# Expert down products cut at 128 rows, with the 48-row pieces of two blocks in the two row halves of the array

## The chip, the cores and the metric

The kernel is one program on one core of one Trainium2 chip. Its engines are TensorE (PE, with its weight loads shown as PEld), VectorE (DVE), ScalarE (ACT), GpSimd (POOL) and SyncE (SP), which run side by side and meet at semaphores. The metric is the device time of one execution in microseconds, the median of several runs.

## What is computed

Four layers follow each other on 2048 tokens of 256 values: a cross attention, a mixture of 64 experts with a shared expert, a second attention and a small mixture of 8. The change is in the second layer, whose reference is, cut to what matters:

```python
def _mlp(x, gw, uw, dw):
    return silu(x @ gw.T) * (x @ uw.T) @ dw.T
rw = _route(x, gate_w, gate_bias)                      # 8 of 64 experts for each token, with weights
expert_out = vmap(lambda gw, uw, dw: _mlp(x, gw, uw, dw))(Wg, Wu, Wd)   # I = 176 inner values each
routed = einsum('eth,te->th', expert_out, rw)
shared = _mlp(x, Sg, Su, Sd)                           # 2 x 176 = 352 inner values
out = routed + shared
```

The down product of an expert is a sum over 176 inner values, and that of the shared expert a sum over 352. The array of PE sums over at most 128 rows in one pass, so each has to be cut. All of it is float32.

## The kernel before

**Blocks.** The tokens of an expert are gathered into half blocks of 64 rows; two half blocks, mostly of one expert or of two neighbours, make a block of 128 rows, and there are 160 blocks (`NRUN`). The first half block of a block (`FIRST`, partitions 0 to 63 of the result) uses the weights of its expert where they were loaded, `wgu` and `wdn`, in one of eight slots (`WSLOT`). The second (`SECOND`, partitions 64 to 127) uses copies, `wguB` and `wdnB`, that DVE and ACT make for each block. A product of `FIRST` takes the left 64 columns of the array and one of `SECOND` the right 64.

**The order on PE.** It is written out by hand, two blocks at a time (`c_group(j)`, j = 0, 2, 4, ...): the down product of block j-3, gate and up products of blocks j and j+1 (`c_up`), the down product of block j-2, then the transposes of the gathered rows of blocks j+2 and j+3 and those of the inner values `hC` of blocks j and j+1. A down product (`c_down`) is four calls: the 176 inner values are cut into two pieces of 88 rows (`IC`), and each piece has one product for `FIRST` and one for `SECOND`, of 64 weight columns by 256 moving columns. In the trace each such call is two matmul records.

**The other engines.** ACT takes the down products out (`c_y_out`, which also scales them), issues the store of the rows (`store_y`), copies the transposed rows (`c_copy_xT`), applies SiLU (`c_gate`) and makes `wdnB` (`second_dn`). DVE multiplies gate and up into `hC` (`c_product`), copies its transpose to `hT` (`c_copy_hT`) and makes `wguB` (`second_gu`). POOL issues the gathers of rows, eight blocks ahead (`gather`), and tells when the weights of a block are there (`weights`, four blocks behind the gather). SP loads the weights of an expert, eight experts ahead, with one DMA for `wgu` and one for `wdn`.

**The shared expert.** Thirteen of the sixteen token tiles go through it while the routing is worked out on DVE (`s_step`: gate and up, the transposes of the tile before, its down product). Three wait until after the last expert block (`l_up`, `l_transpose_h`, `l_down`). Here a tile has 128 rows and one set of weights, so the down product takes all 128 columns; it is four pieces of 88 rows.

Of the kernel before, what the change touches and what calls it, by code (L numbers as in the profile page):

```python
# [14 lines left out]
P = 128  # L15
# [29 lines left out]
IC = I0 // 2  # L45
GU = 2 * I0
NSH = 2
# [58 lines left out]
def bass_flamingo(nc, A, out):  # L106
    with ExitStack() as ctx:  # L107
# [47 lines left out]
        with ExitStack() as region:  # L155
# [6 lines left out]
            scores = s("scores", [P, NT, E0])  # L162
            sfc = s("sfc", [P, NGT, GE])
            t1 = s("t1", [P, NGT, GE])
            t2 = s("t2", [P, NGT, GE])
# [36 lines left out]
            wdnB = s("wdnB", [IC, 2, 2, D])  # L202
# [71 lines left out]
        with ExitStack() as region:  # L274
            s = tensors(region)
            wgu = s("wgu", [P, NSH + WSLOT, DC, GU])
            wdn = s("wdn", [IC, NSH + WSLOT, 2, D])
# [6 lines left out]
            hT = s("hT", [IC, 2, 2, P])  # L284
# [41 lines left out]
        b_trash, b_rw, b_rwd = sem("b_trash"), sem("b_rw"), sem("b_rwd")  # L326
# [8 lines left out]
        c_guB, c_dnB = sem("c_guB"), sem("c_dnB")  # L335
# [84 lines left out]
        FIRST, SECOND = slice(0, HR), slice(HR, P)  # L420
        EARLY_B, LATE_B = slice(0, NT - 4), slice(NT - 4, NT)
# [125 lines left out]
        def _(sp):  # L547
# [20 lines left out]
            sp.dma_start(n1_rows[T:ROWS, :], zero[:]).then_inc(b_trash, 16)  # L568
# [5 lines left out]
            sp.dma_start(wdn[:, 0:NSH, :, :], A["sdn"].rearrange("e (c p) n -> p e c n", p=IC)).then_inc(ld_sh, 16)  # L574
# [8 lines left out]
            def load_dn(e, q):  # L583
                sp.dma_start(wdn[:, NSH + q, :, :], A["wdn"][e].rearrange("(c p) n -> p c n", p=IC)).then_inc(w_ld[q], 16)

            for q in range(WSLOT):
                sp.wait_ge(s_gu, 2 * q + 1)
                load_gu(q, q)
                load_dn(q, q)


            for q in range(WSLOT - 1):
                sp.wait_ge(w_ld[q], 32)
                sp.sem_inc(w_ready, 1)
            sp.wait_ge(b_er, 1)
            with sp.Fori(1, E0 // WSLOT) as i:
                for q in range(WSLOT):
# [4 lines left out]
                    sp.wait_ge(w_ld[last], 32 * i if q == 0 else 32 * i + 32)  # L602
# [3 lines left out]
            sp.wait_ge(w_ld[WSLOT - 1], 32 * E0 // WSLOT)  # L606
# [98 lines left out]
        def _(pool):  # L705
# [32 lines left out]
            power(4, LATE_B)  # L738

# [42 lines left out]
            pool.wait_ge(b_trash, 16)  # L782
            pool.wait_ge(b_st, 16 * XG)
# [56 lines left out]
            pool.wait_ge(const_ready, 3)  # L840
# [162 lines left out]
        def _(act):  # L1003
# [128 lines left out]
            def c_group(j, i, n):  # L1132
# [30 lines left out]
            def l_copy_hT(n):  # L1163
# [4 lines left out]
                act.copy(hT[:], ps[0:IC, 5, :].rearrange("p (f c n) -> p f c n", f=2, c=2)).then_inc(l_hT, 1)  # L1168
# [163 lines left out]
        def _(pe):  # L1332
# [85 lines left out]
            pe.wait_ge(ld_sh, 32)  # L1418
# [1328 lines left out]
```

## Time and profile before

| | |
|---|---|
| median of 3 runs | 1361.5 us (1353.13, 1361.5 and 1361.72) |
| span of the profiled execution, first to last instruction | 1352.5 us; no other time of it is given |
| PE busy | 1232.8 us, 91% of the span |
| DVE, ACT, POOL busy | 913.6, 754.3 and 502.9 us |
| mean granted TensorE clock | 0.974 of full speed |
| HBM | 91 GB/s over the span |

A record of PE has a modelled end, so two neighbouring matmuls seem to overlap; what a matmul costs the engine is the distance from its start to the next start. The busy time of an engine says nothing of whether it is waited for: that is read from the stage in question, from what stood idle before an instruction and what ended it.

### The profile page before, as it was taken

To read this page: it belongs to the slowest core of one execution; us is meant where nothing else is said; L and a number is where in the kernel's file an instruction comes from. 1 tells how busy PE (TensorE), PEld (TensorE's weight loads), DVE (VectorE), ACT (ScalarE), POOL (GpSimd) and SP (SyncE) were. 2 spreads that over 40 slices of the span, in tenths; PEclk is the share of its full clock that TensorE was granted. 3 is DMA by queue.
4 is the path that set the end of the run, shared out by engine and by line. 5 is a ranking of instruction groups with operands and counts; after the bars stand their busy time and mean duration, and the time that the engine had idled before them with its cause. 6 is when DMAs were issued, how large, how long until landed. Compare 5 with 4: busy or idle time off the path is not lost. (4 is left out here: it accounts for less than half of the span.)

```text
span 1352.5 us, 32733 instructions
## 1 busy us (share of the span) xinstructions
PE 1232.8 (91%) x9060; PEld 928.9 (69%) x9062; DVE 913.6 (68%) x2392; ACT 754.3 (56%) x1930; POOL 502.9 (37%) x549
## 2 busy tenths in 40 slices
PE   4999999999999999997578888989878999999998
PEld 3887665555555555554456676767756899999997
DVE  7988857555555555554486876767785766676666
ACT  2444566556565555652447876778764544444443
POOL 1012354333343333424876677774711111011010
PEclk9999999999999999999779999999999999999999
DMA  5013216777576557534432222221200000000000
GB/s 117 0 57 105 78 40 193 228 210 231 174 222 188 172 162 230 179 96 131 131 88 64 67 66 57 63 59 39 96 24 10 16 17 16 16 16 16 8 0 17
DMA packets 99465, 125.02 MB, mean 92 GB/s; under 512 B 28595, under 2 KB 84371, under 8 KB 99347
## 3 DMA queue, kind: packets, MB, share of 16 engines
q1 hardware_dynamic: 62339, 59.05, 15.1%
q0 software_dynamic: 13968, 43.53, 11.6%
q10 hardware_dynamic: 23040, 20.98, 4.6%
q8 instruction: 59, 0.97, 0.3%
q14 instruction: 59, 0.48, 0.1%
HBM read 95.58 MB, written 27.95 MB: 91 GB/s over the span
## 5 line engine op out<-in xcount | busy, mean ns | idle before, releaser
L779 POOL DMA_INDIRECT xg<-n_rows,idx x160 | 163.3, 1021 | 242.3 <-DVE wS L2262 198.7
L1334 PE MATMUL ps<-wgu,xT 128*64 x640 | 202.9, 459 | 0.4 <-ACT xT L1104 0.3
L1334 PE MATMUL ps<-wdn,hT 88*64 (+1 forms) x768 | 199.1, 385 | 4.5 <-ACT hT L1168 2.4
L1334 PE MATMUL ps<-wguB,xT 128*64 128x352 f32 x640 | 202.9, 459 | 0.0
L1212 ACT ACTIVATE pD<-ps,nmx 128x333 f32<-128x333 f32 x256 | 139.2, 547 | 83.7 <-DVE nmx L2443 72.6
L2443 DVE TENSOR_REDUCE nmx<-ps 128x1 f32<-128x333 f32 x256 | 126.2, 496 | 87.1 <-PE ps L1334 86.1
L1334 PE MATMUL ps<-wdnB,hT 88*64 88x256 f32 x640 | 168.4, 386 | 0.0
L1702 PE MATMUL ps<-ident,pD 128*128 128x128 f32 x768 | 135.0, 287 | 35.6 <-DVE pT L2449 33.2
L1334 PEld LDWEIGHTS ps<-wdn,hT 88*64 88x64 f32 (+1 forms) x768 | 104.6, 145 | 74.5 <-issue 43.2
L813 POOL DMA_INDIRECT yg<-y_rows,slotG x128 | 123.3, 963 | 80.8 <-DMA y_rows<-yC 26.4
L1334 PEld LDWEIGHTS ps<-wgu,xT 128*64 128x64 f32 x640 | 87.3, 137 | 85.4 <-issue 73.2
L1702 PEld LDWEIGHTS ps<-ident,pD 128*128 128x128 f32 x768 | 98.7, 146 | 52.5 <-issue 21.0
L1129 ACT ACTIVATE yC<-ps,wS 128x256 f32<-128x256 f32 x160 | 76.0, 475 | 98.4 <-PE ps L1334 97.0
L1334 PE MATMUL ps<-kM,qP 128*128 128x334 f32 x256 | 109.1, 427 | 9.5 <-ACT pD L1212 9.1
L2274 DVE COPY hT<-ps 88x256 f32<-88x256 f32 x160 | 67.0, 419 | 71.9 <-PE ps L1334 67.8
L1300 ACT ACTIVATE sl<-ps 128x256 f32<-128x256 f32 x128 | 48.1, 383 | 104.8 <-PE ps L1334 101.5
L2610 DVE TENSOR_TENSOR gg<-sl,ps 128x256 f32<-128x256 f32 x128 | 52.9, 419 | 77.4 <-ACT sl L1300 76.6
L2262 DVE TENSOR_SCALAR wS<-xg 64x1 f32 x320 | 47.2, 147 | 83.3 <-ACT yC L1129 65.5
L1113 ACT COPY wdnB<-wdn 88x512 f32 x160 | 98.6, 617 | 0.0
L1119 ACT ACTIVATE sg<-ps 128x176 f32<-128x176 f32 x160 | 50.8, 318 | 72.6 <-PE ps L1334 70.5
L1334 PEld LDWEIGHTS ps<-wguB,xT 128*64 128x64 f32 x640 | 87.3, 137 | 0.0
L2255 DVE COPY wguB<-wgu 128x704 f32 x160 | 81.3, 550 | 2.2 <-POOLq L773 2.2
(323 smaller groups left out, 3300.7 us busy)
## 6 DMA issues: line engine op xcount, KB each, us to landing
wgu<-in_wgu SPq DMA_DIRECT2D x64, 352.0 KB
y_rows<-yC ACTq DMA_DIRECT2D x160, 128.0 KB
wdn<-in_wdn SPq DMA_DIRECT2D x64, 176.0 KB
xg<-n_rows,idx POOLq DMA_INDIRECT x160, 3.7
kraw<-in_kD SPq DMA_DIRECT2D x8, 308.0 KB, 2.8
x<-in_x SPq DMA_DIRECT2D x4, 512.0 KB, 5.0
n_rows<-nB SPq DMA_DIRECT2D x4, 512.0 KB, 4.1
yg<-y_rows,slotG POOLq DMA_INDIRECT x128, 4.7
```

The lines of the kernel that those rows point to most:

```text
L779: pool.indirect_dma_start(out=xg[:, b % XS, :], out_offset=None, in_=n1_rows, in_offset=bass.IndirectOffsetOnAxis(ap=idx[:, b:b + 1], axis ...
L813: pool.indirect_dma_start(out=yg[:, q, k, :], out_offset=None, in_=y_rows, in_offset=bass.IndirectOffsetOnAxis(ap=slotG[:, u:u + 1], axis= ...
L1113: act.copy(wdnB[:, n % 2, :, :], wdn[:, bass.ds(slot, 1), :, :].rearrange("p s c n -> p (s c) n")).then_inc(c_dnB, 1)
L1119: act.activation(sg[:, n % 2, :], ps[:, 2 + n % 2, 0:I0], ACT.Silu).then_inc(c_silu, 1)
L1129: act.activation(yC[:, n % YS, :], ps[:, 6 + n % 2, 0:D], ACT.Copy, scale=wS[:, n % XS:n % XS + 1]).then_inc(c_y, 1)
L1212: act.activation(pD[:, k % AHEAD, :], ps[:, score_bank(k), 0:NK1], ACT.Exp, bias=nmx[:, k:k + 1], accum_out=den[:, k // TB // HG1, head_of ...
L1334: return pe.matmul(o, lhsT, rhs, start=start, stop=stop, **kw)
L1702: last = pe.transpose(ps[:, 5 + k % 2, c * P:(c + 1) * P], pD[:, k % AHEAD, at:at + P], ident[:])
L2255: dve.tensor_copy(wguB[:, n % 2, :, :], wgu[:, bass.ds(slot, 1), :, :].rearrange("p s c n -> p (s c) n")).then_inc(c_guB, 1)
L2274: dve.tensor_copy(hT[:, n % 2, :, :], ps[0:IC, 4 + n % 2, 0:2 * P].rearrange("p (c n) -> p c n", c=2)).then_inc(c_hT, 1)
L2443: dve.tensor_reduce(nmx[:, k:k + 1], ps[:, score_bank(k), 0:NK1], AX, ALU.max, negate=True).then_inc(d_mx, 1)
L2610: dve.tensor_tensor(gg[:, f % 2, int(second), :], sl[:, int(second), :], ps[:, f % 4, SEQ:2 * SEQ], ALU.mult).then_inc(f_g2 if second else ...
```

## The change

The 176 inner values of an expert are cut into 128 and 48 instead of 88 and 88. `c_down` now holds only the 128-row piece of a block. The 48-row pieces of two blocks j-3 and j-2 come together in `c_down_rest`, after `c_down(j-2)`: for an even block the piece lies in partitions 64 to 111 and for an odd one in 0 to 47, so that the four products (two blocks, `FIRST` and `SECOND`) stand in four different quarters of the array. `c_dn`, which tells that a down product is done, is raised there for both blocks.

For this the 48 rows of `wdn` are loaded twice, at partitions 0 and 64, and POOL copies them for each block into a new tile `wdnF` of eight places. `wdnB` and `hT` get four places in the place of two. ACT takes out both down products after the gates, in turn with the copies of the transposed rows, and issues both stores at the end. The shared down product is three pieces of 128, 128 and 96 rows in the place of four of 88, and its transposes are three. Of the inner values of an expert block the second transpose has 112 columns (even) or 48 (odd).

The core of the diff:

```diff
-IC = I0 // 2
+IREST = I0 - P
+REST_AT = P // 2
+SHARED_CHUNKS = ((0, P), (P, P), (2 * P, 2 * I0 - 2 * P))
+HTS, FS = 4, 8
+WLOAD = 16 * 4
...
+            wdnB = s("wdnB", [P, HTS, 2, D])
+            wdnF = s("wdnF", [P, FS, D])
...
-            hT = s("hT", [IC, 2, 2, P])
+            hT = s("hT", [P, HTS, 2, P])
...
+        def rest_rows(m):
+            at = REST_AT * (1 - m % 2)
+            return slice(at, at + IREST)
...
-                sp.dma_start(wdn[:, NSH + q, :, :], A["wdn"][e].rearrange("(c p) n -> p c n", p=IC)).then_inc(w_ld[q], 16)
+                sp.dma_start(wdn[:, NSH + q, 0, :], A["wdn"][e][0:P]).then_inc(w_ld[q], 16)
+                for at in (0, REST_AT):
+                    sp.dma_start(wdn[at:at + IREST, NSH + q, 1, :], A["wdn"][e][P:I0]).then_inc(w_ld[q], 16)
...
+            sp.wait_ge(const_ready, 3)
...
+            pool.wait_ge(a_o, NT)
+            pool.wait_ge(a_od, NT)
+            pool.memset(wdn[:, NSH:, 1, :], 0.0).then_inc(const_ready, 1)
...
+                slot = pool.value_load(slot_row[0:1, 0, b:b + 1], min_val=NSH, max_val=NSH + WSLOT - 1)
                 pool.wait_ge(w_ready, need)
                 pool.sem_inc(w_block, 1)
+                if b >= FS:
+                    pool.wait_ge(c_dn, NEARLY + b - FS + 1)
+                pool.tensor_copy(wdnF[:, b % FS, :], wdn[:, bass.ds(slot, 1), 1, :].rearrange("p s n -> p (s n)")).then_inc(c_dnF, 1)
...
-                act.copy(hT[:], ps[0:IC, 4, :].rearrange("p (f c n) -> p f c n", f=2, c=2)).then_inc(s_hT, 1)
+                act.copy(hT_all[:, 0:3 * P], ps[:, 4, 0:3 * P]).then_inc(s_hT, 1)
...
-                act.copy(wdnB[:, n % 2, :, :], wdn[:, bass.ds(slot, 1), :, :].rearrange("p s c n -> p (s c) n")).then_inc(c_dnB, 1)
+                act.copy(wdnB[:, n % HTS, :, :], wdn[:, bass.ds(slot, 1), :, :].rearrange("p s c n -> p (s c) n")).then_inc(c_dnB, 1)
...
-                if inside(j - 3):
-                    c_y_out(j - 3, i, n - 3)
                 if inside(j - 1):
                     second_dn(second[0], j - 1, n - 1)
-                if inside(j - 3):
-                    store_y(j - 3, n - 3)
                 if inside(j):
                     for a in range(GROUP):
                         c_gate(j + a, n + a)
-                if inside(j - 2):
-                    c_y_out(j - 2, i, n - 2)
                 for a in range(GROUP):
+                    if inside(j - 3 + a):
+                        c_y_out(j - 3 + a, i, n - 3 + a)
                     c_copy_xT(j + 2 + a, n + a)
                 if inside(j):
                     second_dn(second[-1], j, n)
-                if inside(j - 2):
-                    store_y(j - 2, n - 2)
+                for a in range(GROUP):
+                    if inside(j - 3 + a):
+                        store_y(j - 3 + a, n - 3 + a)
...
-            def transpose_h(slot, bank, at=0):
-                for c in range(2):
-                    last = pe.transpose(ps[0:IC, bank, at + c * P:at + (c + 1) * P], hC[:, slot, c * IC:(c + 1) * IC], ident[:])
+            def transpose_shared_h(bank):
+                for c, (first, n) in enumerate(SHARED_CHUNKS):
+                    last = pe.transpose(ps[0:n, bank, c * P:(c + 1) * P], h_all[:, first:first + n], ident[:])
+                return last
+            def shared_down(bank):
+                for c, (_, n) in enumerate(SHARED_CHUNKS):
+                    last = mm(ps[:, bank, 0:D], hT_all[0:n, c * P:(c + 1) * P], wdn_all[0:n, c, :], c == 0, c == 2)
                 return last
             def s_down(t, r):
                 after(pe, s_y, t)
                 pe.wait_ge(s_hT, t + 1)
-                for f in range(2):
-                    for c in range(2):
-                        last = mm(ps[:, 6, 0:D], hT[:, f, c, :], wdn[:, f, c, :], f == 0 and c == 0, f == 1 and c == 1)
-                last.then_inc(c_dn, 1)
+                shared_down(6).then_inc(c_dn, 1)
...
             def c_down(m):
-                slot = slots[m]
                 pe.wait_ge(c_dnB, m + 1)
                 pe.wait_ge(c_hT, m + 1)
                 if m == 0:
                     pe.wait_ge(s_y, NEARLY)
                 after(pe, c_y, m - 1)
-                for c in range(2):
-                    mm(ps[FIRST, 6 + m % 2, 0:D], hT[:, m % 2, c, FIRST], wdn[:, bass.ds(slot, 1), c, :], c == 0, c == 1, skip_group_check=True)
-                    last = mm(ps[SECOND, 6 + m % 2, 0:D], hT[:, m % 2, c, SECOND], wdnB[:, m % 2, c, :], c == 0, c == 1, skip_group_check=True)
-                last.then_inc(c_dn, 1)
+                mm(ps[FIRST, 6 + m % 2, 0:D], hT[:, m % HTS, 0, FIRST], wdn[:, bass.ds(slots[m], 1), 0, :], True, False, skip_group_check=True)
+                mm(ps[SECOND, 6 + m % 2, 0:D], hT[:, m % HTS, 0, SECOND], wdnB[:, m % HTS, 0, :], True, False, skip_group_check=True)
+            def c_down_rest(blocks_of):
+                for m in blocks_of:
+                    pe.wait_ge(c_dnF, m + 1)
+                    rows = rest_rows(m)
+                    mm(ps[FIRST, 6 + m % 2, 0:D], hT[rows, m % HTS, 1, FIRST], wdnF[rows, m % FS, :], False, True, skip_group_check=True)
+                for m in blocks_of:
+                    rows = rest_rows(m)
+                    mm(ps[SECOND, 6 + m % 2, 0:D], hT[rows, m % HTS, 1, SECOND], wdnB[rows, m % HTS, 1, :], False, True, skip_group_check=True).then_inc(c_dn, 1)
             def c_transpose_h(m):
                 pe.wait_ge(c_h, m + 1)
                 after(pe, c_hT, m - 1)
-                transpose_h(m % 2, 4 + m % 2).then_inc(c_th, 1)
+                bank = 4 + m % 2
+                pe.transpose(ps[:, bank, 0:P], hC[:, m % 2, 0:P], ident[:])
+                rest = rest_rows(m)
+                pe.transpose(ps[0:rest.stop, bank, P:2 * P], hC[:, m % 2, I0 - rest.stop:I0], ident[:]).then_inc(c_th, 1)
             def c_group(j):
...
                         load_slot(b + 2)
                 if 2 <= j < NRUN + 2:
                     c_down(j - 2)
+                c_down_rest([m for m in (j - 3, j - 2) if 0 <= m < NRUN])
...
+            dve.memset(ps[2 * I0 - 2 * P:P, 4:6, 2 * P:3 * P], 0.0)
...
-                after(dve, c_dn, max(NEARLY, NEARLY + j - 1) if isinstance(j, int) else NEARLY + j - 1)
-                dve.tensor_copy(hT[:, n % 2, :, :], ps[0:IC, 4 + n % 2, 0:2 * P].rearrange("p (c n) -> p c n", c=2)).then_inc(c_hT, 1)
+                after(dve, c_dn, max(NEARLY, NEARLY + j - HTS + 1) if isinstance(j, int) else NEARLY + j - HTS + 1)
+                dve.tensor_copy(hT[:, n % HTS, :, :], ps[:, 4 + n % 2, 0:2 * P].rearrange("p (c n) -> p c n", c=2)).then_inc(c_hT, 1)
```

On PE one pair of blocks stands so before, from the end of the gate and up products on; the two products of `wdn` and two of `wdnB` are the two pieces of block j-2:

```order
L1334 MATMUL ps<-wguB,xT 64x352
L1532 TENSOR_LOAD slot_row
L1532 ISA x2
L1334 ISA
L1334 MATMUL ps<-wdn,hT 64x256
L1334 MATMUL ps<-wdnB,hT 64x256
L1334 ISA
L1334 MATMUL ps<-wdn,hT 64x256
L1334 MATMUL ps<-wdnB,hT 64x256
L1425 MATMUL ps<-ident,xg 128x128 x4
L1430 MATMUL ps<-ident,hC 88x128 x4
```

The second piece is gone from its place, here and in the down product that follows the transposes; the products of `wdnF` and the second `wdnB` are the four 48-row pieces of two blocks, and they stand between the last 128-row piece and the transposes:

```order
L1354 MATMUL ps<-wguB,xT 64x352
L1554 TENSOR_LOAD slot_row
L1554 ISA x2
L1354 ISA
L1354 MATMUL ps<-wdn,hT 64x256
L1354 MATMUL ps<-wdnB,hT 64x256
L1354 MATMUL ps<-wdnF,hT 64x256 x2
L1354 MATMUL ps<-wdnB,hT 64x256 x2
L1445 MATMUL ps<-ident,xg 128x128 x4
L1599 MATMUL ps<-ident,hC 128x128
L1601 MATMUL ps<-ident,hC 112x128
```

On ACT, from the gates of one pair to the second copy of `wdnB` and its store in the next, before:

```order
L1119 ACTIVATE sg<-ps 128x176 x2
L1129 ACTIVATE yC<-ps,wS 128x256
L1104 COPY xT<-ps 128x256 x2
L1113 ISA
L1113 COPY wdnB<-wdn 88x512
L1108 DMA y_rows<-yC 128x256
L414 TENSOR_LOAD slot_row
L1129 ACTIVATE yC<-ps,wS 128x256
L1113 ISA
L1113 COPY wdnB<-wdn 88x512
L1108 DMA y_rows<-yC 128x256
```

And now: both down products leave PSUM right behind the gates, and both stores are issued behind one copy of `wdnB`, ahead of the other:

```order
L1142 ACTIVATE sg<-ps 128x176 x2
L1152 ACTIVATE yC<-ps,wS 128x256
L1127 COPY xT<-ps 128x256
L1152 ACTIVATE yC<-ps,wS 128x256
L1127 COPY xT<-ps 128x256
L1136 ISA
L1136 COPY wdnB<-wdn 128x512
L1131 DMA y_rows<-yC 128x256 x2
L418 TENSOR_LOAD slot_row
L1136 ISA
L1136 COPY wdnB<-wdn 128x512
```

What moved on ACT is the first of the two takings-out: it stood ahead of a copy of `wdnB` and now stands behind the gates of the pair before.

## Rows read from the trace of the kernel before

**Rows 1.** The page, parts 1 and 2: busy time, then 40 slices of the span.
```profile
PE 1232.8 (91%) x9060; PEld 928.9 (69%) x9062; DVE 913.6 (68%) x2392; ACT 754.3 (56%) x1930; POOL 502.9 (37%) x549
...
PE   4999999999999999997578888989878999999998
```

**Rows 2.** Windows view, expert stage: stretch, length, then busy time per engine, PEclk, DMA.
```profile
200.00:300.00 100.00, 100.00 (x760) 57.77 (x758) 63.60 (x198) 59.10 (x152) 40.93 (x42) 1.00 0.71 205
...
500.00:600.00 100.00, 100.00 (x762) 57.75 (x760) 57.59 (x190) 59.48 (x153) 37.95 (x37) 1.00 0.59 176
```

**Rows 3.** Timeline of PE, one pair of blocks: start, us, engine, line, tiles.
```profile
302.41 0.38 PE L1334 MATMUL ps<-wdn,hT 88*64 x1
302.41 0.38 PE L1334 MATMUL ps<-wdnB,hT 88*64 88x256 f32 x1
302.63 0.38 PE L1334 MATMUL ps<-wdn,hT 88*64 x1
...
303.06 0.38 PE L1334 MATMUL ps<-wdn,hT 88*64 x1
...
303.37 0.66 PE L1425 MATMUL ps<-ident,xg 128*128 128x128 f32 x4
303.87 0.60 PE L1430 MATMUL ps<-ident,hC 128*88 128x128 f32 x4
304.40 0.43 PE L1334 MATMUL ps<-wdn,hT 88*64 x1
...
304.66 0.38 PE L1334 MATMUL ps<-wdn,hT 88*64 x1
...
304.88 0.38 PE L1334 MATMUL ps<-wdn,hT 88*64 x1
...
305.31 0.46 PE L1334 MATMUL ps<-wgu,xT 128*64 x1
```

**Rows 4.** Timeline of PE in the second attention layer, four 32-column tiles.
```profile
804.08 1.50 PE L1334 MATMUL ps<-pT,v 77*32 77x256 f32 x24
805.51 0.33 PE L1748 MATMUL ps<-ident,nS 128*128 128x128 f32 x1
```

**Rows 5.** Lines view of POOL: count, busy us and mean ns, then idle before.
```profile
L779 POOL DMA_INDIRECT xg<-n_rows,idx x160 | 163.3, 1021 | 242.3 <-DVE wS L2262 198.7 <-PE ps L1425 19.7 <-SPq L603 14.0
...
L966 POOL COPY maskS<-selE 128x256 f32<-128x256 f32 x24 | 8.7, 403 | 15.4 <-DVE selE L2392 15.4
```

**Rows 6.** Timeline of POOL beside that pair; idle time before in brackets.
```profile
304.21 0.95 POOL L779 DMA_INDIRECT xg<-n_rows,idx  x1 [0.30 <-PE ps L1425]
308.12 1.05 POOL L779 DMA_INDIRECT xg<-n_rows,idx  x1 [2.96 <-DVE wS L2262]
```

**Rows 7.** Timeline of ACT and its queue (ACTq) after that pair.
```profile
306.04 0.60 ACT L1113 COPY wdnB<-wdn 88x512 f32 x1
306.31 0.34 ACTq L1108 DMA_DIRECT2D y_rows<-yC  x1
306.81 0.32 ACT L1119 ACTIVATE sg<-ps 128x176 f32<-128x176 f32 x1 [0.17 <-PE ps L1334]
```

**Rows 8.** Timeline of DVE beside that pair: the copies of gate and up weights.
```profile
303.26 0.97 DVE L2255 COPY wguB<-wgu 128x704 f32 x2
```

**Rows 9.** Windows view, routing beside the shared experts; columns as in Rows 2.
```profile
150.00:160.00 10.00, 8.10 (x40) 5.84 (x38) 9.25 (x16) 5.65 (x14) 5.47 (x6) 1.00 0.19 56
```

**Rows 10.** Timeline of PE in a shared-expert step beside the routing.
```profile
164.68 0.60 PE L1430 MATMUL ps<-ident,hC 128*88 128x128 f32 x4
...
167.05 1.97 PE L1334 MATMUL ps<-wdn,hT 88*128 88x256 f32 x8 [0.58 <-ACT hT L1062]
168.85 2.44 PE L1334 MATMUL ps<-ohB,ohP 128*128 128x160 f16 x32
```

**Rows 11.** Timeline of PE from the last late tile to the next layer.
```profile
633.42 1.99 PE L1334 MATMUL ps<-wdn,hT 88*128 88x256 f32 x8 [0.67 <-ACT hT L1168]
650.34 1.09 PE L1663 MATMUL ps<-ident,nS 128*128 128x128 f32 x4 [14.92 <-DVE nS L2430]
```

**Rows 12.** Timeline of DVE, its first instruction.
```profile
1.90 4.17 DVE L1997 MEMSET kA<- 128x4928 f32 x1 [1.78 <-issue]
```

More of the change, by code:

```diff
@@ L161, in bass_flamingo @@
             gb0 = s("gb0", [P, E0])
[L162 to L165, printed above, removed]
+            with ExitStack() as scratch:
+                scores = tensors(scratch)("scores", [P, NT, E0])
+                sfc, t1, t2 = (tensors(scratch)(n, [P, NGT, GE]) for n in ("sfc", "t1", "t2"))
+            wdnB = s("wdnB", [P, HTS, 2, D])
+            wdnF = s("wdnF", [P, FS, D])
             m1 = s("m1", [P, NGT])
@@ L201, in bass_flamingo @@
             wguB = s("wguB", [P, 2, DC, GU])
-            wdnB = s("wdnB", [IC, 2, 2, D])
             size_b = free0 - nc.sbuf_bytes_remaining
@@ L325, in bass_flamingo @@
         b_st = sem("b_st")
-        b_trash, b_rw, b_rwd = sem("b_trash"), sem("b_rw"), sem("b_rwd")
+        b_rw, b_rwd = sem("b_rw"), sem("b_rwd")
         b_slot = sem("b_slot")
@@ L420, in bass_flamingo @@
         FIRST, SECOND = slice(0, HR), slice(HR, P)
+        h_all = hC[:].rearrange("p f i -> p (f i)")
+        hT_all = hT[:].rearrange("p s c n -> p (s c n)")
+        wdn_all = wdn[:, 0:NSH, :, :].rearrange("p s c n -> p (s c) n")
+        def rest_rows(m):
+            at = REST_AT * (1 - m % 2)
+            return slice(at, at + IREST)
         EARLY_B, LATE_B = slice(0, NT - 4), slice(NT - 4, NT)
@@ L573, in _ @@
             sp.dma_start(wgu[:, 0:NSH, :, :], A["sgu"].rearrange("e (c p) n -> p e c n", p=P)).then_inc(ld_sh, 16)
-            sp.dma_start(wdn[:, 0:NSH, :, :], A["sdn"].rearrange("e (c p) n -> p e c n", p=IC)).then_inc(ld_sh, 16)
+            for c, (first, n) in enumerate(SHARED_CHUNKS):
+                sp.dma_start(wdn_all[0:n, c, :], A["sdn"].rearrange("e i n -> (e i) n")[first:first + n]).then_inc(ld_sh, 16)
             for g in range(XG):
@@ L592, in _ @@
             for q in range(WSLOT - 1):
-                sp.wait_ge(w_ld[q], 32)
+                sp.wait_ge(w_ld[q], WLOAD)
                 sp.sem_inc(w_ready, 1)
@@ L601, in _ @@
                     last = (q - 1) % WSLOT
-                    sp.wait_ge(w_ld[last], 32 * i if q == 0 else 32 * i + 32)
+                    sp.wait_ge(w_ld[last], WLOAD * i if q == 0 else WLOAD * i + WLOAD)
                     sp.sem_inc(w_ready, 1)
@@ L605, in _ @@
                     load_dn(i * WSLOT + q, q)
-            sp.wait_ge(w_ld[WSLOT - 1], 32 * E0 // WSLOT)
+            sp.wait_ge(w_ld[WSLOT - 1], WLOAD * E0 // WSLOT)
             sp.sem_inc(w_ready, 1)
@@ L839, in _ @@
             pool.memset(r0[:], 0.0).then_inc(const_ready, 1)
-            pool.wait_ge(const_ready, 3)
+            pool.wait_ge(const_ready, 4)
             def power_d(phase, s):
@@ L1167, in l_copy_hT @@
                 after(act, l_dn, n)
-                act.copy(hT[:], ps[0:IC, 5, :].rearrange("p (f c n) -> p f c n", f=2, c=2)).then_inc(l_hT, 1)
+                act.copy(hT_all[:, 0:3 * P], ps[:, 5, 0:3 * P]).then_inc(l_hT, 1)
             def l_step(n):
@@ L1415, in _ @@
                     keep_busy(4, 1)
-            pe.wait_ge(ld_sh, 32)
+            pe.wait_ge(ld_sh, 16 * (1 + len(SHARED_CHUNKS)))
             pe.wait_ge(b_sig, NT)
@@ L1426, in transpose_rows @@
                 return last
-            def transpose_h(slot, bank, at=0):
-                for c in range(2):
-                    last = pe.transpose(ps[0:IC, bank, at + c * P:at + (c + 1) * P], hC[:, slot, c * IC:(c + 1) * IC], ident[:])
+            def transpose_shared_h(bank):
+                for c, (first, n) in enumerate(SHARED_CHUNKS):
+                    last = pe.transpose(ps[0:n, bank, c * P:(c + 1) * P], h_all[:, first:first + n], ident[:])
[3 more added lines that the diff above has]
+                    last = mm(ps[:, bank, 0:D], hT_all[0:n, c * P:(c + 1) * P], wdn_all[0:n, c, :], c == 0, c == 2)
                 return last
@@ L1443, in s_transpose_h @@
                 after(pe, s_hT, t)
-                for f in range(2):
-                    last = transpose_h(f, 4, 2 * P * f)
-                last.then_inc(s_th, 1)
+                transpose_shared_h(4).then_inc(s_th, 1)
             def s_step(t, r, i):
@@ L1618, in l_transpose_h @@
                 after(pe, l_hT, n)
-                for f in range(2):
-                    last = transpose_h(f, 5, 2 * P * f)
-                last.then_inc(l_th, 1)
+                transpose_shared_h(5).then_inc(l_th, 1)
             def l_down(n):
@@ L1627, in l_down @@
                 after(pe, l_x, n - 1)
-                for f in range(2):
-                    for c in range(2):
-                        last = mm(ps[:, 6 + n % 2, 0:D], hT[:, f, c, :], wdn[:, f, c, :], f == 0 and c == 0, f == 1 and c == 1)
-                last.then_inc(l_dn, 1)
+                shared_down(6 + n % 2).then_inc(l_dn, 1)
             for n in range(NLATE):
```

11 lines of the change are left out of this document (5 added, 6 removed).

## The prediction

> **What bounds the kernel now.** I read the page first: PE is busy 91% of the span, and its row of slices stands at 9 from the second to the eighteenth [rows 1]. The expert blocks lie in the second half of that, so the windows view comes next. In a stretch of 100 us inside that stage PE is busy for all 100.00, at a granted clock of 1.00 (the 2.4 GHz level), and runs 760 to 762 matmuls; four stretches in a row read alike, and the first and last are shown [rows 2]. A pair of blocks has 40 matmul records (16 of gate and up, 16 of down, 8 transposes), so 760 are 19.0 pairs, and a pair takes 5.26 us. In the same stretches ACT is busy 59 us, DVE 58 to 64, POOL 38 to 41 and the DMA engines 0.59 to 0.71 [rows 2]. Nothing but PE is full here, so this stage is worth what PE's passes are worth. Here are 80 pairs, some 421 us.
>
> The timeline of PE tells what a pass costs [rows 3]. The `FIRST` and `SECOND` products start together (both at 302.41), and the next two 0.22 us later: a slot of 256 columns is 0.215 us, whether one half of the array works in it or both. A down product of a block is four slots, since each call makes two records. Where the form of the array changes, a slot is longer: from the last down slot at 303.06 to the first transpose at 303.37 it is 0.31, and after the transposes the first down slot takes 0.26 (304.40 to 304.66). So a change of form costs about 0.095 ahead of it and 0.045 behind it, 0.14 in all.
>
> **The change, part by part.** *Down products.* Before, the one behind the transposes takes 0.91 us (304.40 to 305.31), the one behind the up products 0.96 (302.41 to 303.37) [rows 3]. After, the first is 0.26 + 0.22 = 0.48, which saves 0.43. The second is two slots of 128 rows and then the four 48-row products. If all four quarters work at once, these are two slots: 0.22, then 0.31 into the new form, 0.26, and 0.31 into the transposes, 1.10 in all, 0.14 more than before. The pair gains 0.29 us, and 80 pairs 23.2.
>
> Two things in this have no row in the trace of before. One is that the four products run side by side although two of them share columns. The nearest row is the value product of the second attention, where 24 matmuls on four column tiles are over in 1.43 us, to the start of the next work (804.08 to 805.51) [rows 4]: six slots of four with one change of form, so four small tiles at once, both records of each, are an ordinary thing. But those tiles are four strips of columns, not two halves of rows. The bounds are two slots (as forecast) and four (the row halves one after the other, 0.43 more). I take two, the row with four tiles being nearer than none. The other is the price of going from 64 columns by 128 rows to 64 by 64. The bounds are 0, as no column tile changes its width, and twice the 0.14 shown; I take 0.14, the price of both changes that are shown. The Trainium skill ("TensorEngine Tiling (Array Packing)", Tiling Modes, key properties) says that changing the tiling mode, and not only the tile, drains the array; by that this change is one that pays, and no run here shows it.
>
> *Transposes of `hC`.* Four a pair as before, of 128 moving columns each; only weight columns differ. Four take 0.44 us at 128 and about as much at 88 columns (303.37 to 303.87 and 303.87 to 304.40, with a change of form in each) [rows 3]. Nothing.
>
> *ACT.* It works 59% of 5.26, 3.1 us a pair [rows 2], and every operation stays, `wdnB` with the same 512 elements on more partitions. Two stores now follow each other; each holds its queue for 0.34, where before one lay under the 0.60 of a copy [rows 7]. So at most 0.7 comes into the open, 3.8 of 4.97 us. The first gate slides back behind them, but what reads it, the transpose of `hC`, comes over 2 us later. Nothing while that stands.
>
> *POOL.* Behind `weights` it gets a copy of 128x256 and a second table load for each block. The same copy elsewhere takes 403 ns [rows 5]; a table load is not a row of POOL, and I estimate it at the 0.30 that stands between two gathers of a pair [rows 6]. POOL idles 2.96 us a pair ahead of the gather that DVE releases [rows 6]; two copies and two loads are 1.4. If each copy also waited for one of DVE's copies (0.97 for two) [rows 8], 2.4. It fits, and gathers run eight blocks ahead. Behind POOL's new wait for `c_dn` stand gathers and later `w_block`; what it asks for is eight blocks old.
>
> *DVE.* The copies of `wguB` end at 304.23 (303.26 and 0.97) [rows 8] and the next gate products start at 305.31 [rows 3]: 1.08 spare. These come 0.43 sooner, which leaves 0.65, and one of POOL's copies, if it held DVE up, takes 0.40. Nothing, but little is left. `hT` with four places takes a wait away.
>
> *SP and the DMAs.* The 48 rows that are loaded twice are 48 KB more beside 528 KB for an expert, 9%, and the busy share of 0.59 to 0.71 [rows 2] has the room. POOL waited for weights 14.0 us in all over 160 gathers [rows 5].
>
> *Shared expert.* Two slots of eight and one transpose of four go, 0.43 + 0.11. Up to 159 us DVE is the bound (9.25 of 10) [rows 9] and it gives nothing. In the three steps between the one-hot products PE runs through but for 0.58 us behind ACT's `hT` [rows 10]; I take 0.4 for each (0 if ACT then holds, 0.6 with its shorter copy), and 0.5 for the thirteenth tile, which lies at the start of the expert stage: 1.7. The three late tiles end near 635.4, and PE then waits 14.92 us for DVE [rows 11], behind the gathers of expert rows: nothing.
>
> *Ends.* The last block's down product now waits until the rest of the two before it is taken out, 0.5 as an estimate, between the 0.32 and the 0.60 of ACT's operations [rows 7]. The clear of PSUM at DVE's start is 256 elements, 0.2 at the 4.17 us for 4928 of the row there [rows 12].
>
> *Sum.* -23.2 - 1.7 + 0.5 + 0.2 = -24.2 us on the span of 1352.5, which gives 1328.3. The median of the runs stands 9.0 above that span (the lowest 0.6 above); I carry the change over: 1361.5 - 24.2 = **1337 us**.
>
> **The rivals.**
> - *The row halves run one after the other* (slower). Place: the four 48-row products. Price: two more slots a pair, 0.43 - 0.29 = +0.14, 80 times, less 1.0 from the rest: +10, **1372 us**. It decides from 1.4 slots more than the forecast's two. For it: no row with two tiles in the same columns. Against: two tiles and four are seen to share a slot [rows 3, 4].
> - *The four products go through in strict order.* If a record that waits for its own tile holds all behind it, four products of two records each need five slots (the first alone, three shared, the last alone): 3 x 0.215 more, +0.355 a pair, +27, **1389 us**. The rows speak against it: by the same rule the second `FIRST` record would hold the first `SECOND` one, which starts with it at 302.41 [rows 3]. The Trainium skill ("TensorE: Matmul & The Clock Gate", Part 3) states this rule, that matmuls start and end strictly in program order; the trace does not agree if the two records of a call stand together.
> - *No price for the new form.* Then the pair gains the full 0.43: -34.4 - 1.0, **1326 us**.
> - *A hand-off becomes the bound.* PE is now 0.29 faster, and what had room may not: DVE's `wguB` held by POOL, ACT's gates behind two stores, POOL's chain. A pair then takes between 4.97 and 5.26 us; halfway, **1349 us**.
>
> **How the numbers follow.** The forecast gets 0.62, no price 0.12, row halves in turn 0.12, a hand-off 0.10, strict order 0.02, and 0.02 for something else that makes it slower. The forecast's own range is 1326 to 1347, from 0.1 us a pair and the 8 us between runs. The range of 1322 to 1358 takes in the first, second and fourth and leaves out the row halves and the two small ones. About 1% (13.6 us) is what a measurement of this kernel can tell from no change. Faster by more: 0.62 + 0.12 + a third of the hand-off, 0.77. Within: most of the row halves (1372 is 0.8% above) and the rest of the hand-off, 0.18. Slower by more: 0.05.
>
> **What would show it.** In the windows of the expert stage PE still full, and pairs of 4.97 us (19.0 of them in 94.5 us). In PE's timeline four starts together with a `wdnF` product among them, twice, and about 0.31, 0.26 and 0.31 around them; four slots there are the first rival, five the second, 0.215 the third. A hand-off would show as idle time ahead of up or down products, with ACT or DVE as what ended it. The forecast is wrong if the four don't share slots, or if PE idles in that stage.

## The result, and the profile after

The changed kernel takes **1336.2 us** (median of 4 runs, 1334.1 to 1338.6), against 1361.2 us for the kernel before: a ratio of 0.983, 95% interval 0.981 to 0.986. In a second session it took 1337.0 us against 1356.1, ratio 0.985 (0.983 to 0.987). The forecast was 1337.0 us, in a range of 1322 to 1358. The profiled execution took 1334.1 us, with a span of 1332.4.

The page of the changed kernel, parts 1 and 2 (the lines that answer to [rows 1]):

```profile
PE 1211.2 (91%) x9012; PEld 894.4 (67%) x9014; DVE 919.3 (69%) x2393; ACT 745.1 (56%) x1930; POOL 574.3 (43%) x710
...
PE   5999989999999999993678989888978999999998
```

PE has lost 21.6 us of busy time, POOL has gained 71.4. The windows view of the expert stage, with the columns of [rows 2]:

```profile
200.00:300.00 100.00, 100.00 (x798) 52.77 (x796) 68.18 (x206) 60.30 (x159) 59.96 (x85) 1.00 0.76 223
...
400.00:500.00 100.00, 100.00 (x804) 53.07 (x802) 61.50 (x201) 60.76 (x160) 59.12 (x80) 1.00 0.67 192
```

PE is still full, at a granted clock of 1.00. A pair still has 40 matmul records, so 798 to 804 of them are some 20 pairs where 19 stood [rows 2]. PE's timeline over one pair, from its end to the end of the next one and two products on (start, us, engine, line, tiles; the answer to [rows 3]):

```profile
451.04 0.66 PE L1445 MATMUL ps<-ident,xg 128*128 128x128 f32 x4
...
454.62 0.46 PE L1354 MATMUL ps<-wgu,xT 128*64 x1
...
454.92 0.38 PE L1354 MATMUL ps<-wdn,hT 128*64 x1
...
455.13 0.38 PE L1354 MATMUL ps<-wdn,hT 128*64 x1
...
455.45 0.43 PE L1354 MATMUL ps<-wdnF,hT 48*64 48x256 f32 x2
455.46 0.43 PE L1354 MATMUL ps<-wdnB,hT 48*64 48x256 f32 x2
455.71 0.38 PE L1354 MATMUL ps<-wdnF,hT 48*64 48x256 f32 x2
455.73 0.38 PE L1354 MATMUL ps<-wdnB,hT 48*64 48x256 f32 x2
456.04 0.66 PE L1445 MATMUL ps<-ident,xg 128*128 128x128 f32 x4
...
457.06 0.43 PE L1354 MATMUL ps<-wdn,hT 128*64 x1
...
457.33 0.38 PE L1354 MATMUL ps<-wdn,hT 128*64 x1
...
457.55 0.46 PE L1354 MATMUL ps<-wgu,xT 128*64 x1
```

From transposes to transposes is 5.00 us (451.04 to 456.04), where it was 5.27 (411.20 us over 78 pairs, in the table below). Two neighbours of the kernel before:

```profile
603.95 0.66 PE L1425 MATMUL ps<-ident,xg 128*128 128x128 f32 x4
...
609.23 0.66 PE L1425 MATMUL ps<-ident,xg 128*128 128x128 f32 x4
```

In the changed kernel, at 455.45, four products start together, two of `wdnF` and two of `wdnB`; their second records follow at 455.71: two slots. Around them stand 0.32 (455.13 to 455.45), 0.26 and 0.33 (455.71 to 456.04). The down product behind the transposes takes 0.49 (457.06 to 457.55).

Where the 20.2 us between the two profiled spans came from, by the starts of instructions in PE's timelines (us):

| stretch | before | after | difference |
|---|---|---|---|
| start to the last routing product of the gate | 111.62 | 111.38 | -0.24 |
| to the first one-hot product (shared expert beside the routing) | 47.46 | 43.13 | -4.33 |
| to the last one-hot product | 27.33 | 28.92 | +1.59 |
| to the first transposes of a whole pair | 12.00 | 12.62 | +0.62 |
| to the last transposes of rows (78 pairs) | 411.20 | 390.29 | -20.91 |
| to the first product of the next attention | 42.50 | 43.56 | +1.06 |
| to the end | 700.43 | 702.47 | +2.04 |

The 78 pairs gave 20.9, where 78 times 0.29 is 22.6; the whole gave 20.2, where 24.2 was forecast. Two stretches did not go by the forecast: the shared expert gave 4.3 us in a stretch where nothing was expected and lost 1.6 in the one where the gain was to be, and the layers behind took 2.0 more.

### The profile page after: what moved, and what is told of

Its sections match the earlier page's. It is cut to its first block and busy times, and to the rows that moved or that the text cites. A ratio compares the mean times of both kernels' runs of the same rounds, so it can differ in the third digit from the quotient of the medians.

```text
span 1332.4 us, 33579 instructions
## 1 busy us (share of the span) xinstructions
PE 1211.2 (91%) x9012; PEld 894.4 (67%) x9014; DVE 919.3 (69%) x2393; ACT 745.1 (56%) x1930; POOL 574.3 (43%) x710
## 5 line engine op out<-in xcount | busy, mean ns | idle before, releaser
L803 POOL DMA_INDIRECT xg<-n_rows,idx x160 | 158.9, 993 | 128.5 <-DVE wS L2291 105.2
L1354 PE MATMUL ps<-wdnB,hT 48*64 48x256 f32 (+1 forms) x640 | 147.4, 397 | 0.0
L1136 ACT COPY wdnB<-wdn 128x512 f32 x160 | 101.2, 633 | 58.9 <-issue 50.9
L1354 PE MATMUL ps<-wdn,hT 128*64 (+2 forms) x416 | 123.4, 391 | 4.9 <-ACT hT L1188 2.1
L2284 DVE COPY wguB<-wgu 128x704 f32 x160 | 92.0, 616 | 3.5 <-POOLq L794 3.5
L1354 PEld LDWEIGHTS ps<-wdn,hT 128*64 128x64 f32 (+2 forms) x416 | 54.5, 148 | 53.5 <-issue 46.2
L2297 DVE TENSOR_TENSOR hC<-sg,ps 128x176 f32<-128x176 f32 x160 | 53.0, 337 | 51.5 <-ACT sg L1142 48.4
L797 POOL COPY wdnF<-wdn 128x256 f32 x160 | 72.4, 453 | 35.7 <-issue 18.2
```

The source lines that it names most:

```text
L797: pool.tensor_copy(wdnF[:, b % FS, :], wdn[:, bass.ds(slot, 1), 1, :].rearrange("p s n -> p (s n)")).then_inc(c_dnF, 1)
L803: pool.indirect_dma_start(out=xg[:, b % XS, :], out_offset=None, in_=n1_rows, in_offset=bass.IndirectOffsetOnAxis(ap=idx[:, b:b + 1], axis ...
L1136: act.copy(wdnB[:, n % HTS, :, :], wdn[:, bass.ds(slot, 1), :, :].rearrange("p s c n -> p (s c) n")).then_inc(c_dnB, 1)
L1354: return pe.matmul(o, lhsT, rhs, start=start, stop=stop, **kw)
L2284: dve.tensor_copy(wguB[:, n % 2, :, :], wgu[:, bass.ds(slot, 1), :, :].rearrange("p s c n -> p (s c) n")).then_inc(c_guB, 1)
L2297: dve.tensor_tensor(hC[:, n % 2, :], sg[:, n % 2, :], ps[:, 2 + n % 2, I0:GU], ALU.mult).then_inc(c_h, 1)
```

## The experiments

**Do four quarters share slots?** Two kernels keep everything but the row half: the 48-row pieces of both blocks lie in partitions 0 to 47. They differ in the order of issue.

```diff
         def rest_rows(m):
-            at = REST_AT * (1 - m % 2)
+            at = 0
```

In the first the four calls stand block by block, so that both quarters are taken up at once by each block:

```diff
                     mm(ps[FIRST, 6 + m % 2, 0:D], hT[rows, m % HTS, 1, FIRST], wdnF[rows, m % FS, :], ...)
-                for m in blocks_of:
-                    rows = rest_rows(m)
                     mm(ps[SECOND, 6 + m % 2, 0:D], hT[rows, m % HTS, 1, SECOND], wdnB[rows, m % HTS, 1, :], ...)
```

Expected of it:

> The changed kernel, but the 48-row pieces of both blocks lie in partitions 0 to 47, so the two blocks use the same two quarters of the array; the four products are issued block by block (first and second half block of j-3, then of j-2). Theory (the gain is that four quarters share two slots): four slots in the place of two, 0.43 us more a pair, 5.43 us, and 80 times that on 1336: 1370 us, slower than the kernel before by 9. Rival (the gain came from elsewhere, the order on ACT, the four places of hT or the shared expert): a pair within 0.1 of 5.00 and about 1337 to 1344.

It took 1368.9 us, ratio 1.008 (1.005 to 1.011). PE's timeline of the four products:

```profile
452.14 0.43 PE L1354 MATMUL ps<-wdnF,hT 48*64 48x256 f32 x1
...
452.40 0.38 PE L1354 MATMUL ps<-wdnF,hT 48*64 48x256 f32 x1
...
452.62 0.38 PE L1354 MATMUL ps<-wdnF,hT 48*64 48x256 f32 x1
...
452.83 0.38 PE L1354 MATMUL ps<-wdnF,hT 48*64 48x256 f32 x1
...
453.15 0.66 PE L1445 MATMUL ps<-ident,xg 128*128 128x128 f32 x4
```

Four slots, a pair of 5.42 us, and the kernel is slower than before. The copies by POOL, the order on ACT, the four places of `hT` and the shared expert are all still those of the changed kernel; so none of them alone makes the stage faster, and the shared slots do.

The second keeps the order of the changed kernel, both `FIRST` and then both `SECOND`. Expected:

> As the kernel with both blocks in the same row half, but issued in the changed kernel's own order: the two products of FIRST, then the two of SECOND, so that the second call needs the quarter of the first. Theory (a call starts once its quarter is free, but no call passes one that is issued ahead of it): 2 slots for the first alone, 2 for the next two together, 2 for the last, 6 slots, 0.86 us more a pair than 5.00, 1405 us. Rival A (each quarter has a queue of its own and calls pass each other): four slots, 5.43 us, 1370. Rival B (strict order by record): seven slots, 1.07 more, 1422 us.

It took 1370.3 us, ratio 1.010 (1.007 to 1.013), a pair of 5.42. My theory of this run failed, and its rival A holds. PE's timeline, of that kernel:

```profile
451.91 0.43 PE L1354 MATMUL ps<-wdnF,hT 48*64 48x256 f32 x1
451.92 0.43 PE L1354 MATMUL ps<-wdnB,hT 48*64 48x256 f32 x1
452.18 0.38 PE L1354 MATMUL ps<-wdnF,hT 48*64 48x256 f32 x1
452.19 0.38 PE L1354 MATMUL ps<-wdnB,hT 48*64 48x256 f32 x1
452.39 0.38 PE L1354 MATMUL ps<-wdnF,hT 48*64 48x256 f32 x1
452.40 0.38 PE L1354 MATMUL ps<-wdnB,hT 48*64 48x256 f32 x1
```

The second `wdnF` call is issued ahead of the first `wdnB` call, yet `wdnB` starts at 451.92 and that `wdnF` call at 452.39, once its quarter is free. A call that waits for its quarter lets later ones pass.

**What does a change of form cost?** The four products are moved from behind the last down product to behind the one that follows the transposes, so that the array goes from 128 rows to 64 and back to 128 between products that are of one form.

```diff
                 if j >= 3:
                     c_down(j - 3)
+                c_down_rest([m for m in (j - 4, j - 3) if 0 <= m < NRUN])
...
                 if 2 <= j < NRUN + 2:
                     c_down(j - 2)
-                c_down_rest([m for m in (j - 3, j - 2) if 0 <= m < NRUN])
```

On ACT `c_y_out` of j-4 and j-3 stand ahead of the gates. Expected:

> The changed kernel, but the four 48-row products (now of blocks j-4 and j-3) stand behind the down product that follows the transposes, ahead of the up products, in the place of standing between the last down product and the transposes; ACT takes both results out ahead of the gates. The work is the same, and the array changes between 128 and 64 rows twice a pair in the place of once (before, one of the two changes was one into the transposes that is paid in any case). Theory (every change of form costs about 0.14 us): a pair of 5.14, 80 times 0.14 on 1336: 1347 us. Rival A (a change that leaves the 64-column tiles as they are is free, and the 0.14 over the full gain of the pair has another cause): 5.00 and 1336. Rival B (ACT's two takings-out ahead of the gates hold the gates): idle time of PE ahead of up products or transposes, over 5.2 us.

It took 1348.9 us, ratio 0.995 (0.993 to 0.997), a pair of 5.15. PE's timeline:

```profile
449.77 0.43 PE L1355 MATMUL ps<-wdnF,hT 48*64 48x256 f32 x2
...
450.04 0.38 PE L1355 MATMUL ps<-wdnF,hT 48*64 48x256 f32 x2
...
450.37 0.51 PE L1355 MATMUL ps<-wgu,xT 128*64 x1
...
450.71 0.46 PE L1355 MATMUL ps<-wgu,xT 128*64 x1
...
451.01 0.46 PE L1355 MATMUL ps<-wgu,xT 128*64 x1
```

Out of the 64-row form it is 0.33 instead of 0.22, and the first up slot is 0.34 instead of 0.30 (450.37 to 450.71, then to 451.01). One more change costs 0.15 us a pair (5.15 - 5.00), and these two distances are all of it (0.11 + 0.04). Rival A falls: a change that leaves the 64 columns as they are is paid in full.

**Is POOL's copy covered, and how far?** In one kernel the copy is left out from the ninth block on, in another it is made twice.

```diff
-                pool.tensor_copy(wdnF[:, b % FS, :], ...).then_inc(c_dnF, 1)
+                if b < FS:
+                    pool.tensor_copy(wdnF[:, b % FS, :], ...).then_inc(c_dnF, 1)
...
-                    pe.wait_ge(c_dnF, m + 1)
+                    if m < FS:
+                        pe.wait_ge(c_dnF, m + 1)
```

> The changed kernel, but POOL copies the 48-row weights into wdnF only for the first eight blocks; for the other 152 the products read what then stands there, so the routed part of the output is left wrong. Everything else, POOL's waits and table loads too, stays. Theory (PE's slots and changes of form set the pair, POOL is covered): a pair stays at 5.00 us, total 1334 to 1338, while the mean of DVE's copies of gate and up weights falls from 616 ns back towards 550. Rival (the copies hold DVE or a gather and so set part of the pair, which is why it is 5.00 and not 4.97): a pair of 4.97 or less, 1331 to 1334.

It took 1335.1 us, ratio 0.983 (0.980 to 0.986), and a pair stays at 5.00. The copies of gate and up weights on DVE, first in the changed kernel (with those into `wdnF` and the gathers), then without POOL's copies (lines view: count, busy us, mean ns, then idle before):

```profile
L2284 DVE COPY wguB<-wgu 128x704 f32 x160 | 92.0, 616 | 3.5 <-POOLq L794 3.5
...
L797 POOL COPY wdnF<-wdn 128x256 f32 x160 | 72.4, 453 | 35.7 <-issue 18.2 <-PE ps L1354 8.5 <-SPq L620 4.9
...
L803 POOL DMA_INDIRECT xg<-n_rows,idx x160 | 158.9, 993 | 128.5 <-DVE wS L2291 105.2 <-PE ps L1445 12.7 <-issue 9.0
```

```profile
L2286 DVE COPY wguB<-wgu 128x704 f32 x160 | 79.0, 533 | 4.9 <-POOLq L794 4.9
```

So POOL's copy makes each of DVE's longer by 83 ns (616 - 533), some 13 us of DVE in all, and costs the kernel nothing.

The other kernel adds the same copy again:

```diff
+                pool.wait_ge(c_dnF, 2 * b + 1)
+                pool.tensor_copy(wdnF[:, b % FS, :], ...).then_inc(c_dnF, 1)
...
-                    pe.wait_ge(c_dnF, m + 1)
+                    pe.wait_ge(c_dnF, 2 * m + 2)
```

> The changed kernel with POOL's copy into wdnF made twice, the second after the first. POOL then works some 0.9 us more a pair, about 75% of it. Theory (POOL has room and only the copies of DVE grow): a pair of 5.00 and 1334 to 1339, DVE's wguB at 0.65 to 0.70 us. Rival (the chain of POOL, or DVE beside it, is near its end): a pair over 5.05 and PE idle ahead of the up products or the transposes of xg, 1342 or more.

It took 1346.9 us, ratio 0.992 (0.990 to 0.994). Here the theory falls and the rival holds, though not as written: most pairs are still 5.00, but the mean is 5.10, and ten of them are over 5.15, up to 8.86. The view of waits names the hand-off (us in total, times, longest), for DVE from 200 to 590, and then for PE from 190 to 600:

```profile
DVE wguB L2286 <- POOLq L794: 95.4, 78, 3.9
```

```profile
PE ps L1356 <- DVE wguB L2286: 3.0, 3, 2.2
```

POOL tells ahead of each copy that the weights of a block are there (line 794); with two copies this comes late for DVE, which waits in nearly every pair, and now and then PE waits for DVE, 2.2 us in the pair of 8.86. DVE's copies themselves are shorter here, 553 ns, so it is not their length that holds PE. By the starts, that same product behind `wguB` is 2.37 us late in the pair of 8.86, and late by 0.08 to 0.76 in six of the other nine. The wait has a second price: from 474.50 to 477.90, right behind it, the granted clock is 0.52, and the remaining 1.4 us of that pair go with it.

**What is the shared expert worth?** The changed kernel with four pieces of 88 rows and four transposes a tile:

```diff
-SHARED_CHUNKS = ((0, P), (P, P), (2 * P, 2 * I0 - 2 * P))
+SHARED_CHUNKS = tuple((c * I0 // 2, I0 // 2) for c in range(4))
...
```

> The changed kernel with the shared expert put back to four pieces of 88 rows and four transposes a tile; the expert blocks as changed. Theory: the 1.7 us that the forecast gave to the shared expert are lost, mostly in the three steps between the one-hot products and in the thirteenth tile; the pair stays at 5.00; 1337 to 1339 us. Rival (part of the 3 us by which the changed kernel was ahead at the start of the expert stage came from the earlier routing and not from these steps): under 1 us. Rival B (the shared steps before the one-hots count too): over 3 us.

It ran beside the changed kernel again:

> The changed kernel once more, beside the next three on the same chip: 1334 to 1338 us, a pair of 5.00.

They took 1338.7 us (ratio 0.986, 0.984 to 0.988) and 1337.0 (0.985, 0.983 to 0.987). The difference of 1.7 is the forecast's number, but the intervals overlap, and the total doesn't settle it. The stretches do. To the first one-hot product it is 47.45 us with four pieces and 43.1 to 43.6 in the nine profiles with three. Over the one-hots it is 27.19 with four and 28.2 to 29.5 with three. So three pieces are ahead by 3.9 to 4.3 and give back 1.0 to 2.3. The forecast had its 1.7 in the second stretch and the thirteenth tile, so its size is near and its place is not.

**What next?** If the passes of PE set the pair, another pass less must show. The 48 inner values of two blocks are put side by side, so that one transpose turns both:

```diff
-            hC = s("hC", [P, 2, I0])
+            hC = s("hC", [P, EVEN_AT + I0])       # EVEN_AT = P + P // 2
...
-                bank = 4 + m % 2
-                pe.transpose(ps[:, bank, 0:P], hC[:, m % 2, 0:P], ident[:])
-                rest = rest_rows(m)
-                pe.transpose(ps[0:rest.stop, bank, P:2 * P], hC[:, m % 2, I0 - rest.stop:I0], ident[:]).then_inc(c_th, 1)
+                if m % 2:
+                    pe.transpose(ps[0:REST_AT + IREST, 4, P:2 * P], hC[:, P:EVEN_AT + IREST], ident[:]).then_inc(c_th, 1)
+                    pe.transpose(ps[:, 5, 0:P], hC[:, 0:P], ident[:]).then_inc(c_th, 1)
+                else:
+                    pe.transpose(ps[:, 4, 0:P], hC[:, EVEN_AT + IREST:EVEN_AT + I0], ident[:])
...
```

> The changed kernel with the 48 inner values of two blocks side by side in one tile, so that one transpose of 112 columns turns both (rows 0 to 47 and 64 to 111), three transposes of inner values a pair in the place of four; DVE's product of an even block becomes two instructions, and its copy of an odd block's hT is half as wide. Theory (PE's passes alone set the pair): 0.11 us less a pair, 4.89, and 80 times that: 1327 to 1328 us. Rival A (the one transpose waits for both products, and DVE's extra instruction lies ahead of it): PE idle ahead of the transposes, 5.00 or more, 1336 and up. Rival B (with less work on PE another engine is the bound): between, with idle time on PE ahead of up products.

It took 1332.3 us, ratio 0.982 (0.980 to 0.984), 4.8 us less than the changed kernel beside it, with intervals that overlap; 80 times 0.11 would be 8.8. The pair settles it: it is 4.96, and only at either end of the stage 4.89. So PE's passes alone do not set the pair; the total lies between, as in rival B, but not with the wait that rival B names. PE's and ACT's timelines of it:

```profile
454.94 0.27 PE L1602 MATMUL ps<-ident,hC 128*128 128x128 f32 x1
455.21 0.42 PE L1356 MATMUL ps<-wdn,hT 128*64 x1
```

```profile
454.49 0.47 ACT L1154 ACTIVATE yC<-ps,wS 128x256 f32<-128x256 f32 x1 [0.85 <-PE ps L1356]
```

From the last transpose to the down product is 0.27 (0.20 in the changed kernel, 456.86 to 457.06). PE shows no idle time for it, since the ends of its records are modelled; the gap has to be read from the starts. What that product waits for is the bank of the block two earlier, which ACT leaves at 454.96. In the changed kernel the fourth transpose covered that.

The last kernel gives the down products a third bank. For that all three transposes of a pair go into bank 4, and DVE copies them at once:

```diff
+        def y_bank(m):
+            return 6 if m % 2 == 0 else 7 if m % 4 == 1 else 5
...
-                after(pe, c_y, m - 1)
+                after(pe, c_y, m - 3 if m % 2 else m - 1)
...
-                    pe.transpose(ps[:, 5, 0:P], hC[:, 0:P], ident[:]).then_inc(c_th, 1)
+                    pe.transpose(ps[:, 4, 2 * P:3 * P], hC[:, 0:P], ident[:]).then_inc(c_th, 1)
...
+                dve.tensor_copy(hT_all[:, 2 * (n % HTS) * P:(2 * (n % HTS) + 3) * P], ps[:, 4, 0:3 * P]).then_inc(c_hT, GROUP)
```

> The kernel with three transposes of inner values a pair, which ran at 4.96 us a pair and not at 4.89: the first down product behind the transposes asks for the bank of PSUM from which ACT takes out the product of two blocks earlier, and that taking-out is now late. Here all three transposes of a pair go into one bank (one copy of 384 columns by DVE in the place of two), and the bank that comes free is a third one for down products, so that an odd block needs the bank of four blocks earlier. Theory (that wait is the 0.07): 4.89 us a pair, 1326 to 1328 us. Rival (the wait is another one at the same place, the copy of the transposed rows or of the inner values): 4.93 to 5.0 and 1331 or more.

It took **1326.2 us**, ratio 0.975 (0.973 to 0.978), the fastest of all, with a pair of 4.89. Its timelines at the same place:

```profile
455.50 0.27 PE L1607 MATMUL ps<-ident,hC 128*128 128x128 f32 x1
455.70 0.43 PE L1360 MATMUL ps<-wdn,hT 128*64 x1
```

```profile
455.05 0.47 ACT L1158 ACTIVATE yC<-ps,wS 128x256 f32<-128x256 f32 x1 [0.85 <-PE ps L1360]
```

The gap is 0.20 again, though ACT is no earlier against PE. The joined copy of DVE has no part in it, since the product's own `hT` was copied a pair earlier. The product starts 0.18 after ACT is done with the bank of two blocks earlier (455.52), where the one that asked for it started 0.25 after (454.96 to 455.21).

## Why the prediction was right

*What bounds the kernel.* Right: PE was full before and is full after, at the same clock, and what was added to it moved the pair by its own time (two slots 0.42, a change of form 0.15). A pass taken away did so only when a bank was free: 0.04 of 0.11, then 0.11.

*Two slots for the four products.* Right. The choice between two and four slots was made from column tiles [rows 4]; with both blocks in one row half the pair came to 5.42, 0.15 over that of before, where that rival has 0.14, and the total to 13.0 us over that of before in its session (1368.9, 1355.8), where it has 10. So its price was right, and the mechanism that decides is the quarter.

*The price of the form.* Forecast 0.14 from the change into the transposes and out of them, measured 0.15 by an added change, and 0.32 and 0.33 stand around the four where 0.31 was said. The Trainium skill ("TensorEngine Tiling (Array Packing)", Tiling Modes, key properties) has a change of tiling mode drain the array; the trace agrees in that a change is paid, 0.15 us here, and doesn't show whether the array drains. The rival with no price falls.

*The pair.* Forecast -0.29, measured -0.27 to -0.28 (5.27 to 5.00). The rest of 0.02 is in the slots around the four products; their starts stand 7 ns apart one by one, so that the last of the four starts some 20 ns behind the first. Over 80 pairs 22 us, for 23.2.

*Strict order.* Falls, and by more than was argued: in the run with both blocks in one half a later call overtakes an earlier one. The Trainium skill ("TensorE: Matmul & The Clock Gate", Part 3) states that matmuls start and end strictly in program order; the trace does not agree for calls on different tiles.

*POOL, DVE, ACT.* Nothing was forecast, and nothing was lost. The copy takes 453 ns (estimate 403), and the idle time ahead of the gathers fell from 242 us [rows 5] to 128.5, 1.4 us a pair, the lower end of 1.4 to 2.4. That little is left was right too: a second copy already costs 10 us, in the main by the way POOL tells DVE late and the clock behind that wait, and not by DVE's slower copies.

*The shared expert.* The sum of -1.7 came near the -2.7 (-4.3 + 1.6) by two errors against each other. The step that failed reads "Up to 159 us DVE is the bound (9.25 of 10) and it gives nothing". It rested on the window 150 to 160 [rows 9], which takes in the wait for the first one-hots. Windows that end ahead of it (columns as in [rows 2]), first before the change:

```profile
147.00:152.00 5.00, 5.00 (x26) 3.42 (x25) 4.71 (x25) 2.01 (x6) 1.86 (x4) 1.00 0.70 192
152.00:157.00 5.00, 5.00 (x23) 3.80 (x23) 5.00 (x6) 2.01 (x6) 3.43 (x4) 1.00 0.11 37
157.00:162.00 5.00, 2.98 (x25) 2.25 (x24) 4.38 (x6) 4.57 (x5) 1.29 (x2) 0.83 0.00 0
```

and after it:

```profile
148.00:153.00 5.00, 4.82 (x21) 3.32 (x19) 4.76 (x13) 2.10 (x8) 2.83 (x4) 1.00 0.26 88
153.00:158.00 5.00, 2.77 (x23) 2.34 (x24) 5.00 (x8) 4.35 (x5) 1.55 (x2) 0.73 0.00 0
158.00:163.00 5.00, 4.89 (x21) 3.28 (x20) 5.00 (x8) 1.17 (x4) 0.17 (x1) 0.58 0.00 0
```

PE was full up to 157 us, and DVE nearly so (4.71, then 5.00). The products that count for the routing stand behind shared steps in PE's queue, so shorter steps bring them, and DVE, forward: eight steps lie there, of 4.00 us each where they were 4.54, and eight times 0.54 are the 4.3. The run with four pieces, which is otherwise the changed kernel, is back at 47.45, so the shorter steps are the cause. One step of PE, before and after:

```profile
118.59 1.89 PE L1334 MATMUL ps<-wdn,hT 88*128 88x256 f32 x8
...
123.13 1.89 PE L1334 MATMUL ps<-wdn,hT 88*128 88x256 f32 x8
```

```profile
118.24 1.46 PE L1354 MATMUL ps<-wdn,hT 128*128 128x256 f32 x6
...
122.24 1.46 PE L1354 MATMUL ps<-wdn,hT 128*128 128x256 f32 x6
```

The three steps between the one-hots were to give 0.4 each and gave 0.09, as these rows of PE show:

```profile
173.21 1.84 PE L1354 MATMUL ps<-ohB,ohP 128*128 128x160 f16 x24
175.37 0.71 PE L1354 MATMUL ps<-ohB,ohP 128*128 128x160 f16 x8 [0.32 <-ACT ohP L1090]
...
180.79 1.84 PE L1354 MATMUL ps<-ohB,ohP 128*128 128x160 f16 x24
```

From one group of one-hots to the next is 7.58 us (173.21 to 180.79), where it was 7.67: PE now waits 0.32 for ACT's `ohP` ahead of the last eight. At the first one-hots PE came early and idled, and there the granted clock was at the lower level (1.2 GHz) for longer: 0.73 and 0.58 in the two windows. The clock shows 6.8 us at that level in this profile and 3.4 before; in two later profiles with three pieces (without POOL's copies, and with three banks) it was 3.4 as well, and the one-hots took 28.3 and 28.2. So some 0.7 of the 1.6 went with the clock; the other 0.9 is there without it. In those two profiles PE waits 3.9 us in all for ACT's `ohP` between 150 and 191 us, against 2.0 before and 2.0 with four pieces: 1.9 more, which takes up the 1.6 that three steps, each 0.54 shorter, would give. So what makes the one-hots holds PE there; the rest of the 0.9 stays open.

*The ends.* The tail of the stage was forecast at 0.5 and is 0.7 (from the last transposes to the last expert's products 8.41 before, 9.09 after); PE waits there for ACT's `yC`, 0.19 and 0.78 us.

*The layers behind.* No term was given for them, and the profile has +2.0, with a mean clock of 0.967 against 0.974 over the whole execution. The nine other profiles have 702.4 to 705.6 us there against one of before with 700.4, whose span of 1352.5 is near the shortest of its executions (1350.8 to 1361.1 in the later sessions). The mean clock of the kernel before was 0.968 to 0.974 in 30 later executions, on average 0.972, and that of the changed one 0.962 to 0.970 in 9, on average 0.967. So the change seems to go with a lower clock, for which the forecast had no term; why stays open.

*The total.* That 1336.2 lies 0.8 from the forecast's 1337.0 is in part luck. The terms came to 24.2 and the profiled spans differ by 20.2: the pairs gave some 1 us less, the shared expert 1 more, and the layers behind, the way into the pairs and the ends cost some 4 more than the 0.7 that was put there. The base of 1361.5 was high by about as much: in the three later sessions the kernel before took 1355.8, 1356.1 and 1359.0, and beside the second of these the changed one was 19.1 less.

## What to carry to other kernels

Where PE is full, count its slots by the starts of its records, and pack products that use half the rows into the four quarters; one change of form a group (0.15 us) is paid by two saved slots (0.43), so keep such products together. Before a bound is named from a stretch, take a window that ends ahead of the next wait: one that reaches into the wait makes the engine that is full look half idle. When a pass is taken away, ask which bank or buffer it had covered; the next gain here lay in a bank and not in an engine.

## What the runs showed of the hardware

Four 64 x 64 tiles run float32 products side by side in the time of one, with starts 7 ns apart. A product that waits for its tile doesn't hold those behind it that go to other tiles (451.92 ahead of 452.39). A change between 128-row and 64-row tiles of the same width costs 0.15 us, about as much as one between widths (0.14, [rows 3]). And POOL's copies beside DVE's made DVE's longer, 616 ns where they took 533 without them.
